# A spline stage that shares its gathering with GpSimd, and a reordered start of local attention

## The reference

```python
xn = (x - mu) * rsqrt(var + eps) * gamma + beta        # tokens N x 256
scores = sign(xn) @ cluster_sigs.T, sign(xn) @ tile_sigs.T
tile_idx = best of the 64 tiles in the best of 8 clusters
x_slice = the 4 features of that tile                   # gathered by token
mn, mx = min and max of x_slice over all tokens that chose the tile
u = clip((x_slice - mn) / (mx - mn + 1e-8), 0, 1 - 1e-6)
b, s = spline_bases, spline_slopes at (tile_idx, j, floor(16 u))
x = x + scattered((b + s * x_local) * output_scale[tile_idx])
```

## Time and profile before

| | |
|---|---|
| three runs | 1044.77, 1045.63, 1046.61 us; median 1045.63 |
| profiled execution | 1046.12 us, span 1044.3 us |
| busy in the span | PE 987.1, VectorE 772.3, ScalarE 701.9, GpSimd 330.7 us |
| mean granted TensorE clock | 0.982 of full speed |

### The profile page before, as it was taken

How to read it: one execution, slowest core, us unless ns; L and a number is a source line. 1 busy time by engine, 2 the same in 40 slices (tenths; PEclk the granted TensorE clock), 3 DMA queues, 4 the chain that set the end, 5 groups by cost and what they waited for, 6 DMA issues and landing times. The chain is left out here.

```text
span 1044.3 us, 19330 instructions
## 1 busy us (share of the span) xinstructions
PE 987.1 (95%) x6896; PEld 818.3 (78%) x6925; DVE 772.3 (74%) x1525; ACT 701.9 (67%) x1959; POOL 330.7 (32%) x276
## 2 busy tenths in 40 slices
PE   7999999999999999999999988699999989899997
PEld 3898888888998899889988866577777789774444
DVE  5798867667676676776757989899998644567774
ACT  5888876777767776776662358487788535448882
POOL 1343333322333233323310120054545310106672
PEclk9999999999999999999999998999999999899999
DMA  7322000000000001000205000000000000018652
GB/s 211 94 61 61 1 2 1 2 1 1 2 1 1 1 2 36 2 1 1 82 16 132 1 1 1 1 2 2 1 2 2 2 1 2 8 51 277 217 180 81
DMA packets 31841, 40.21 MB, mean 39 GB/s; under 512 B 8193, under 2 KB 23297, under 8 KB 31745
## 3 DMA queue, kind: packets, MB, share of 16 engines
q1 hardware_dynamic: 31744, 38.98, 11.9%
HBM read 36.74 MB, written 2.23 MB: 37 GB/s over the span
## 5 line engine op out<-in xcount | busy, mean ns | idle before, releaser
L349 POOL TENSOR_TENSOR roped_q<-roped_q,sin_q 128x512 f32<-128x512 f32 x64 | 82.0, 1281 | 302.3 <-DVE sin_q L494 302.3
L1664 ACT ACTIVATE win_P<-banks,win_neg_max 128x128 f32<-128x128 f32 x256 | 91.4, 382 | 27.6 <-DVE win_neg_max L1740 27.3
L349 POOL TENSOR_TENSOR roped_k<-roped_k,sin_k 128x512 f32<-128x512 f32 x64 | 83.2, 1301 | 46.6 <-DVE sin_k L494 46.6
L403 ACT ACTIVATE P<-banks,neg_max 128x128 f32<-128x128 f32 x256 | 90.5, 372 | 6.9 <-DVE neg_max L519 6.6
L437 ACT ACTIVATE oT_hi<-banks,bv_col 128x512 fp32r<-128x512 f32 x64 | 44.1, 690 | 74.2 <-PE banks L667 74.2
L1601 POOL TENSOR_TENSOR win_P<-win_P,win_inv 128x512 f32<-128x512 f32 x64 | 66.9, 1046 | 70.4 <-DVE win_inv L1745 70.3
L412 ACT ACTIVATE sin_k<-banks 64x512 f32<-64x512 f32 x128 | 76.0, 594 | 11.6 <-PE banks L37 10.1
L522 DVE SCALAR_TENSOR_TENSOR oT_lo<-banks,bv_col,oT_hi 128x512 fp32r<-128x512 f32 x64 | 47.9, 749 | 42.6 <-ACT oT_hi L437 42.0
L412 ACT ACTIVATE sin_q<-banks 64x512 f32<-64x512 f32 x128 | 76.0, 594 | 2.9 <-PE banks L37 0.7
L629 PE MATMUL banks<-WO_lo,oT_hi 128*128 128x256 f32 x256 | 72.9, 285 | 0.0
L493 DVE SCALAR_TENSOR_TENSOR roped_k<-banks,qk_bias,cos 128x512 f32<-128x512 f32 x64 | 48.0, 750 | 33.2 <-ACT sin_k L412 33.2
(11 more groups left out here) (428 smaller groups left out, 3141.2 us busy)
## 6 DMA issues: line engine op xcount, KB each, us to landing
ret_V<-moe_gate_rows SPq DMA_DIRECT2D x16, 512.0 KB, 4.8
ctx<-moe_gate_rows SPq DMA_DIRECT2D x16, 512.0 KB, 5.2
X<-in_x SPq DMA_DIRECT2D x4, 512.0 KB, 6.6
stage<-in_wqT SPq DMA_DIRECT2D x4, 512.0 KB, 4.1
stage<-in_wvT SPq DMA_DIRECT2D x4, 512.0 KB, 5.9
stage<-in_woT SPq DMA_DIRECT2D x4, 512.0 KB, 4.3
ctx<-in_ctxT SPq DMA_DIRECT2D x4, 512.0 KB, 5.8
out<-X SPq DMA_DIRECT2D x8, 256.0 KB, 2.4
```

Source lines behind the costliest of these rows:

```text
L349: nc.gpsimd.tensor_tensor(roped[w][:, p, :], roped[w][:, p, :], sin_part[w][:], ALU.add).then_inc(roped_sum[w], 1)
L403: ins = nc.scalar.activation(P[:, i, :], SC[:, i * 128:(i + 1) * 128], ACT.Exp, bias=neg_max[:, r % 2, i:i + 1], accum_out=exp_sum[:, r % ...
L1664: ins = nc.scalar.activation(P[:, h % 2, s, i, :], SC[2 * (h % 2) + s][:, i * 128:(i + 1) * 128], ACT.Exp, bias=neg_max[:, h % 2, at:at + ...
```

## The change

Spline:

- GpSimd makes the norms of groups 2 and 3; PE, ScalarE and VectorE wait for its count `xn_pool` where they read them.
- The gathering of the first half is divided: GpSimd takes batches 0 to 5 (lengths 1536, 768, 384 and 192), VectorE batches 6 and 7 (512, 256, 128, 64). The reduction of the half stands behind the second half's gathering.
- GpSimd makes both weight splits (the former L1372 and L1385).
- ScalarE and PE take the hot columns of half one before the signs and scores of group 3.
- Bounds: the largest value is negated, and minima of both are taken together, in one series of VectorE; the sixteen operations of ScalarE are gone.

Local attention: before the ticks VectorE finishes batches 2 to 4 instead of 2 to 6, with the splits of the first pair and the second pair's norm earlier; batches 5 to 11 follow one in each of the ticks 0, 1, 2, 4, 5, 6, 7. The statistics of batches 4 to 7 are finished in tick 2 instead of 0, and GpSimd's power for them stands behind the products of tick 1 instead of before all ticks.

The diff, cut to its core:

```diff
+        SHARED, OWN = slice(0, 6), slice(6, HALF)
+
+        def gather_some(eng, link, tensor_tensor, some, done):
+            n = some.stop - some.start
+            link(tensor_tensor(wide[:, some, :].rearrange("p b (t j) -> p (b t) j", j=W), XN[:, some, :].rearrange("p b (t j) -> p (b t) j", j=W),
+                               hot[:, some, :].rearrange("p b (t a) -> p (b t) a", a=1).broadcast_to([128, n * NT, W]), ALU.mult))
+            for m in (128, 64):
+                link(tensor_tensor(wide[:, some, 0:m], wide[:, some, 0:m], wide[:, some, m:2 * m], ALU.add))
+            tensor_tensor(wide[:, some, 0:32], wide[:, some, 0:32], wide[:, some, 32:64], ALU.add).then_inc(done, 1)
...
             @block.gpsimd
             def _(pool):
...
+                normalise(2)
                 pool.wait_ge(stat, 8)
                 nc.gpsimd.tensor_tensor(rstd12[:, LATE], var12[:, LATE], minus_half[:, LATE], ALU.pow).then_inc(rstd12_ready, 1)
+                pool.wait_ge(rstd12_ready, 1)
+                normalise(3)
                 nc.gpsimd.tensor_tensor(rstd[:, LATE], var_eps[:, LATE], minus_half[:, LATE], ALU.pow).then_inc(rstd_ready, 1)
+                pool.wait_ge(hot_ready, 1)
+                gather_some(pool, pool_link, nc.gpsimd.tensor_tensor, SHARED, pool_gathered)
+                pool.wait_ge(win_rounded, 1)
+                nc.gpsimd.tensor_tensor(kept["win_qk_lo"][:], w["win_wqk"][:], kept["win_qk_hi"][:].bitcast(F32), ALU.subtract).then_inc(win_split, 1)
+                pool.wait_ge(win_rounded, 2)
+                nc.gpsimd.tensor_tensor(kept["win_w_lo"][:], w["win_w_in"][:], kept["win_w_hi"][:].bitcast(F32), ALU.subtract).then_inc(win_split, 1)
...
             @block.scalar
...
                 take_signs(2)
+                take_hot(0)
+                take_hot(1)
                 take_signs(3)
...
-                act.wait_ge(high_known, 1)
-                for b in range(B):
-                    place_high(b)
                 for g in range(NG):
                     take_hot_b(g)
+                act.wait_ge(xn_pool, 2 * GROUP)
...
             @block.vector
...
-                normalise(2)
-                dve.wait_ge(rstd12_ready, 1)
-                dve.wait_ge(stat, n)
-                normalise(3)
...
-                gather(0)
+                gather_some(dve, link, TT, OWN, own_gathered)
                 choose(1)
+                dve.wait_ge(xn_pool, 2 * GROUP)
                 gather(1)
+                dve.wait_ge(own_gathered, 1)
+                dve.wait_ge(pool_gathered, 1)
+                link(reduce(xs[:, half(0), :], wide[:, half(0), 0:32].rearrange("p b (t j) -> p b j t", j=W), AX.X, ALU.add))
...
-                reduce(lo_hi[:, 1, :], xs[:], AX.X, ALU.max).then_inc(high_known, 1)
+                reduce(lo_hi[:, 1, :], xs[:], AX.X, ALU.max, negate=True)
                 link(reduce(lo_hi[:, 0, :], xs[:], AX.X, ALU.min))
                 dve.wait_ge(off_ready, 2)
-                link(TT(extreme[:, 0], off[:], over(lo_hi[:, 0, :], NT), ALU.add))
-                extreme_of(0, ALU.min)
-                dve.wait_ge(win_rounded, 1)
-                TT(kept["win_qk_lo"][:], w["win_wqk"][:], kept["win_qk_hi"][:].bitcast(F32), ALU.subtract).then_inc(win_split, 1)
-                dve.wait_ge(high_placed, B)
-                extreme_of(1, ALU.max)
+                link(TT(extreme[:], off[:].rearrange("p (a b) n -> p a b n", a=1).broadcast_to([128, 2, B, NT]),
+                        lo_hi[:].rearrange("p a (b n) -> p a b n", n=1).broadcast_to([128, 2, B, NT]), ALU.add))
+                for m in (8, 4, 2):
+                    link(TT(extreme[:, :, 0:m], extreme[:, :, 0:m], extreme[:, :, m:2 * m], ALU.min))
+                TT(tile_ext[:], extreme[:, :, 0], extreme[:, :, 1], ALU.min).then_inc(ext_ready, 1)
...
-                dve.wait_ge(win_rounded, 2)
-                TT(kept["win_w_lo"][:], w["win_w_in"][:], kept["win_w_hi"][:].bitcast(F32), ALU.subtract).then_inc(win_split, 1)
...
             @block.tensor
...
+                transpose_x(2)
+                score_tiles(1)
+                score_tiles(2)
+                transpose_hot(0)
+                transpose_hot(1)
+                transpose_x(3)
+                score_tiles(3)
```

and in local attention:

```diff
+        FINISHED = 5, 6, 7, None, 8, 9, 10, 11, None, 12, None, 13, None, 14, None, 15
...
-                    if h in (7, 15):
-                        part = 2 + h // 8
+                    if h in (1, 7, 15):
+                        part = 1 + (h + 1) // 8
...
                 finish_part(0)
+                split_q(0)
+                normalise(1)
+                split_k(0)
                 finish_batch(4)
-                normalise(1)
-                finish_batch(5)
-                split_q(0)
-                finish_batch(6)
-                split_k(0)
...
-                    if p == 2 and m + 2 < PAIRS + CROSS:
+                    if p == (2 if m > 0 else 3) and m + 2 < PAIRS + CROSS:
                         normalise(m + 2)
-                    if h == 0:
-                        finish_batch(7)
-                        finish_part(1)
-                    if h % 2 == 1 and h < 16:
-                        finish_batch(8 + h // 2)
-                    if h in (8, 16):
-                        finish_part(1 + h // 8)
+                    if h < len(FINISHED) and FINISHED[h]:
+                        finish_batch(FINISHED[h])
+                    if h in (2, 8, 16):
+                        finish_part({2: 1, 8: 2, 16: 3}[h])
```

More of the change, by code:

```diff
@@ L1188, in phase_spline @@
         found_ready = sem("sp_found_ready")
[L1189 to L1190 removed]
         ext_ready = sem("sp_ext_ready")
+        xn_pool = sem("sp_xn_pool")
+        pool_chain = sem("sp_pool_chain")
+        pool_gathered = sem("sp_pool_gathered")
+        own_gathered = sem("sp_own_gathered")
         ext_transposed = sem("sp_ext_transposed")
@@ L1214, in _, with pool_link, normalise @@
             def _(pool):
+                count = [0]
+                def pool_link(ins):
+                    count[0] += 1
+                    ins.then_inc(pool_chain, 1)
+                    pool.wait_ge(pool_chain, count[0])
+                def normalise(g):
+                    for b in range(GROUP * g, GROUP * (g + 1)):
+                        nc.gpsimd.tensor_scalar(XN[:, b, :], X[:, b, :], mean[:, b:b + 1], rstd12[:, b:b + 1], ALU.subtract, ALU.mult).then_inc(xn_pool, 1)
+                normalise(2)
                 pool.wait_ge(stat, 8)
                 nc.gpsimd.tensor_tensor(rstd12[:, LATE], var12[:, LATE], minus_half[:, LATE], ALU.pow).then_inc(rstd12_ready, 1)
+                pool.wait_ge(rstd12_ready, 1)
+                normalise(3)
                 nc.gpsimd.tensor_tensor(rstd[:, LATE], var_eps[:, LATE], minus_half[:, LATE], ALU.pow).then_inc(rstd_ready, 1)
+                pool.wait_ge(hot_ready, 1)
[4 more added lines that the diff above has]
+                nc.gpsimd.tensor_tensor(kept["win_w_lo"][:], w["win_w_in"][:], kept["win_w_hi"][:].bitcast(F32), ALU.subtract).then_inc(win_split, 1)
                 pool.wait_ge(next_stat, 2 + 7)
@@ L1252, in take_found @@
                     nc.scalar.activation(flat(found[:, 2 * p:2 * p + 2, :]), bank[4 + 2 * (p // 4) + p % 2][:, 0:2 * TABW], ACT.Copy).then_inc(found_ready, 1)
-                def place_high(b):
-                    nc.scalar.activation(extreme[:, 1, b, :], off[:, b, :], ACT.Identity, bias=lo_hi[:, 1, b:b + 1], scale=-1.0).then_inc(high_placed, 1)
                 def residual(b):
@@ L1266, in _ @@
                 for i in range(2):
-                    for g in (2 * i, 2 * i + 1):
-                        take_hot(g)
+                    if i == 1:
+                        take_hot(2)
+                        take_hot(3)
                     make_off(i)
@@ L1427, in transpose_x @@
                 def transpose_x(g):
-                    pe.wait_ge(xn_ready, GROUP * (g + 1))
+                    if g < 2:
+                        pe.wait_ge(xn_ready, GROUP * (g + 1))
+                    else:
+                        pe.wait_ge(xn_pool, GROUP * (g - 1))
                     wait(pe, signs_ready, KD * (g - 1))
@@ L1480, in _ @@
                 score_tiles(0)
-                for g in range(1, NG):
-                    if g + 1 < NG:
-                        transpose_x(g + 1)
-                    score_tiles(g)
+                transpose_x(2)
[5 more added lines that the diff above has]
+                score_tiles(3)
                 for i in range(2):
-                    for g in (2 * i, 2 * i + 1):
-                        transpose_hot(g)
+                    if i == 1:
+                        transpose_hot(2)
+                        transpose_hot(3)
                     for p in range(4 * i, 4 * i + 4):
@@ L1592, in power @@
                     return nc.gpsimd.tensor_tensor(rstd[:, some], var_eps[:, some], minus_half[:, some], ALU.pow)
-                for part in range(2):
```

(4 more changed lines are left out.)

16 lines of the change are left out of this document (5 added, 11 removed).

## The result

The changed kernel took **1052.07 us** (median of 6 runs, 1048.60 to 1052.74), the kernel before 1045.43 us (6 runs on the same chip, 1044.77 to 1049.86). The ratio is 1.0046, with a 95% interval of 1.0026 to 1.0065: slower, by about 5 us. The profiled execution was the shortest of the six, 1048.6 us (span 1046.8). Its stage in question begins at 612.7, 2.2 us earlier than before, behind identical code, and its cross-attention, identical too, is 1.8 us shorter; so I compare within stages. Local attention took 177.26 us before and 177.55 after. Together these are +6.7 us.

A forecast was written before the change was run, and what follows sets the result against it. VectorE's series was taken to bound the spline and its total local attention, with GpSimd holding VectorE up on SBUF. 1046.1 + 4.9 (spline) - 0.5 (local attention) = 1050.5 us, range 1042.5 to 1054.

The forecast's parts named there:

- Part 1: Spline, norms of batches 8 to 15 on GpSimd at 0.45 us each: 0 (-0.4 to +1.3).
- Part 2: Spline, first half's gathering divided: GpSimd's products and sums hold VectorE's, second choice of tiles starts later: +1.7 us.
- Part 3: Spline, query/key weight split on GpSimd (2.4 us) catches VectorE's SBUF-only operations in the second choice: +1.3 us.
- My rule: A VectorE operation with two SBUF inputs waits until a GpSimd one that reads SBUF is nearly over.
- Part 4: Spline, put-off reduction ahead of the columns' use, +0.6; value/output split on GpSimd holds VectorE's first short product, +2.1 us.
- Part 5: Spline, bounds in one series -0.7; transposes after its end +0.35, split moved off VectorE -0.4 us.
- Part 6: Local attention's front: scoring starts 2.3 us sooner, mostly lost again in the ticks: -0.5 us (-2.3 to +1).
- (a): Rival: long GpSimd operations let VectorE in between; 1044.5 us, no change; chance 0.18.
- (d): Rival: the splits miss VectorE by the order of requests, giving back 2.8 us; 1047.7 us; chance 0.10.
- (c): Rival: dearer GpSimd gathering product and norms (0.776 us), +1 to +2.5; 1052.5 us; chance 0.12.
- (b): Rival: local attention's ticks keep the head start, batches 5 and 6 filling idle time, -2.3; 1042.7 us; chance 0.20.

The follow-up runs named there:

- e3: Changed kernel with both weight splits back on VectorE; ran once, 1047.90 us, stage 51.45 us against 53.2 in the changed kernel.
- e4: Changed kernel with local attention's order as before and the spline as changed; ran once, 1050.50 us, ninth maximum at 50.75.
- e6: Kernel before with only the bounds in one series, both splits on VectorE; 1045.33 against 1047.34 us, ratio 0.9987 (0.9970 to 1.0003).
- e7: Kernel before plus one unused GpSimd product of 1536 elements; ran once, stage 49.8 us against 46.8 in the kernel before.
- e5: Kernel before with only local attention's new order, 3 rounds; 1045.18 against 1047.34 us, ratio 0.9973 (0.9959 to 0.9987).
- e9: The kernel of e5 timed again in 5 rounds; 1044.48 against 1046.59 us, ratio 0.9980 (0.9966 to 0.9993).
- e11: Changed kernel with norms, gathering and both splits back on VectorE, keeping the new PE and ScalarE order and bounds; ran once, 1048.04 us, stage 50.6.
- e8: Changed kernel with GpSimd's 1536-element gathering product in six pieces of 256; ran once, stage 52.9 us, 0.2 less than the changed kernel.
- e12: Kernel before with new local attention order, one-series bounds, and query/key split on GpSimd in two timed halves; 1046.12 against 1045.70 us, ratio 0.9996.
- e2: Changed kernel with all of the first half's gathering back on VectorE; ran once, 1048.19 us, stage 51.7.

## Why the prediction was right, and where it was wrong

The forecast was slower, 1050.5 us, on the ground that GpSimd's operations hold up VectorE's. The time was 1052.07, and the collisions were where it said. Against the kernel before, the forecast was +4.4 us and the ratio gives +4.8. By its steps, in the profile after:

- **Part 1 (0, bounded by -0.4 and +1.3): +2.4.** The step that failed. The mis-sized term is the norm on GpSimd: 1.28 and 1.21 us (5.12 and 4.83 for four), nearly three times the cast that I took and well above the 0.776 that I called dear. VectorE's first eight norms took 3.35 us together instead of 2.83, the 0.5 that I had reckoned, though GpSimd worked beside all of them. But GpSimd's queue grew to 12 us, and I had its two powers done before the first choice ends; `rstd` came 1.2 us late. The 2.4 is the norms' alone: at the faster clock of e3 and e4 the first choice begins 0.8 sooner and the wait for `rstd` is 1.0 longer, and the shift starts at the same 12.2 to 12.3. The wait is the term that I had put at nothing.
- **Part 2 (+1.7): +1.4.** Right in course: all is held until GpSimd's 1536 elements are through, in 2.91 us (reckoned: 3.1). The caught operation is the 16-element shift and not the product behind it, so VectorE's own product was short (0.68) where I had named 3 us as the sign.
- **Part 3 (+1.3): +1.6.** The 0.20 us product was caught, the comparison not; 2.35 us for 1024 elements (2.4). That product has one tensor input. My rule was worded for two, and by it alone the product would have gone free; the step came out because I counted with it anyway.
- **Part 4 (+0.6 and +2.1): +0.7 and +1.2.** The reduction is as said. The product waited half as long as forecast, because ScalarE's second half took 3.7 us instead of 4.7 from its first rounding to its last column (PE's clock 1.00 instead of 0.63 in it), so GpSimd started 1.1 us before VectorE was there. e4 shows how loose this is: with GpSimd's start 1.8 us later against VectorE's series, the price was 2.05.
- **Part 5 (-0.75): -0.95.** As said; and in e6's profile it is worth nothing alone.
- **Part 6 (-0.5): +0.3.** First maximum -3.1 (-2.3), lead gone by the ninth, as said. I had counted 1.1 us of collisions. The larger term is plainer: ticks 4 to 7 finish four batches in after and two before, at 1.3 us each, and these ticks grew by 2.2 in every trace. The sign of the sum isn't settled, since the ninth maximum varies by 2 to 3 us between traces of the same code.

The stages' sum is +6.7 where I had +4.4. Part 1 alone is as large as the difference; that the other misses (+0.8, +0.3, -0.3, -0.8, -0.2) cancel is luck. Two prices of rivals were also added up wrongly: (a) takes 0.9 for bounds and split where Part 5 has 0.75, and (d) gives back 2.8 where Parts 3 and 4 have 3.4. **Rival (a)** is ruled out by e7: at three times the length that was in evidence, the hold is still the whole operation. The Trainium skill says so in "SBUF — State Buffer", section "Who interferes with whom"; here a 2.92 us operation held up an operation of 0.17 us for 2.73. GpSimd's norms don't follow it, though they read SBUF: VectorE's comparison took 0.69 us beside one, as without, and the measurement decides. Rivals (c) and (d) were both partly true: the norms were dearer, and where splits met VectorE was chance. Rival (c), dearer norms, names the term that failed, and its 1052.5 is nearer to the measured time than my own number. Rival (b)'s mechanism didn't happen: the 2.2 us that ticks 4 to 7 grow by stand in every trace with the new order, although that order alone ran 2 us faster in e5 and e9.

**Open**: why e5 and e9 run at a higher granted clock, with which their 2 us go. Their traces agree with before's in every stage within 0.8 us but for the starts of the stages behind unchanged code, which move by up to 2 us from run to run. One profile of one execution can't show 0.2%. Open too is why GpSimd's two-tensor operations hold VectorE for their whole length and its norms don't, and what of the new order makes PE's clock fall. And I didn't try e11 with the old order of ScalarE and PE together with GpSimd's work, so the cost of that order inside the full change isn't measured.

## What to carry to other kernels

Before giving work of a full VectorE to GpSimd, list every operation that VectorE runs in that window on SBUF alone and that isn't a reduction, however small and also with one tensor input: each may wait for the end of a GpSimd operation on two tensors, so the price is set by GpSimd's longest piece and by who comes first, not by how much moved. Pieces let VectorE in (e8), and work placed where VectorE reads PSUM or reduces holds nothing (e12), but neither brought this kernel more than 0.2 us, as the next collision or the next engine took the gain. Check what queues behind the moved work on GpSimd itself, small powers above all. And undo the parts together as well as one by one: savings of single undoings (5.6 us here, 4.6 at a like clock) may stand on a bound that only appears when all are undone (2.6 us).

## What the runs showed of the hardware that I had not expected

- GpSimd takes 1.2 us for a subtraction and product with two values per partition on 128x256; the cast of that size is 0.447, a product of two tensors 0.69 (e8).
- These norms of GpSimd don't hold VectorE for their length (1.2 us). In after, e2, e3, e4 and e8 the comparison of two SBUF inputs (512 elements) takes 0.69 us while a norm runs, and the 64-element product 0.20 to 0.40. What holds it are GpSimd's operations on two tensors.
- The hold shows as a long duration of the waiting operation and never as idle time. It catches a 16-element operation with two tensor inputs (2.81) and those with one tensor and constants (2.90 in e7, 1.86 in after), and it didn't catch a reduction that reads SBUF (0.60 beside the split in e2) nor an operation that reads PSUM (0.69 beside the split in after). GpSimd is held the same way when VectorE comes first (4.42 instead of 2.37).
- Six queued pieces of GpSimd let VectorE in after each (0.54, 0.67, 1.20), so the lock is given up between operations although GpSimd's next is ready.
- PE's granted clock in the first 5 us of the stage was 1.00 or 0.66, with the new and with the old order, and moved the first choice by 1 us (6.8 or 7.9). A difference below that in one profile says nothing of the edit. Later in the stage the clock follows the order: the same projection took 1.99 us in all seven traces with the old one and 3.3 to 3.8 in all seven with the new one.
